# Token products of three tiles with the contraction outside, loads in sixths, low parts on GpSimd, another order of calls

## The chip, the cores and the metric
The kernel runs on one core of a Trainium2 chip, as one launch. The metric is the device time of the launch in microseconds, the median of several runs. The program is one block in which each engine (TensorE, VectorE, ScalarE, GpSimd, SyncE) has its own list of instructions, runs them strictly in order, and waits on semaphores for the others.

## The reference, cut to what matters
A small vision tower: 16 images of 96x96x3, 37 tokens each (36 patches and a class token), 592 rows of 256.

```python
tokens = einsum('bnd,ed->bne', patchify(x, 16), W) + b      # 768 -> 256
h = concatenate([cls, tokens], axis=1) + pos_embedding
n = layernorm(h)
q, k, v = n @ Wq, n @ Wk, n @ Wv            # 8 heads of q, 4 of k and v, 128 wide
q, k = rope(q), rope(k)                     # x * cos + rotate_half(x) * sin
h = h + softmax(causal(q @ k.T * scale)) @ v @ Wo
n = layernorm(h)
probs = softmax(n @ router_w.T); gate = top 4 of 16, the rest 0
h = h + sum over 2 shared experts of gelu(n @ up.T) @ down.T
      + sum over 16 routed experts of gate * (gelu(n @ up.T) @ down.T)
```

## The kernel before
The 592 rows are five tiles of 128 rows (the last has 80). For attention they are six groups of 3, 3, 2 images (111, 111, 74 rows, twice), and for the rope two halves of 296 rows.

**Products with high and low parts.** Apart from the token products, the scores and the products with v, every matmul is made of three: a float32 operand is split into a high part (ScalarE copies it to the float32r type) and a low part (what the rounding left, a subtraction), and `three` adds high x high, high x low, low x high. So each weight and each activation needs a ScalarE copy and a subtraction before TensorE can use it. The subtraction of the attention weights is `qkv_low` on VectorE (L635), four pieces of 128x1024; `qkv_high` on ScalarE (L408) comes first. That of the expert weights is `low_parts` on GpSimd (L372), after `high_parts` on ScalarE (L479).

**Tokens.** `x_sb` holds the patches transposed (six contraction chunks of 128), `wp_sb` the weights (six chunks). `tokens(i)` multiplies tile i over all six chunks, `tokens_added(i)` adds position, bias and class token through a product with `aux_pick` and `aux_parts`, which VectorE prepares in `split_added` (L812 to L817) when `aux_sb` and `auxs_sb` have landed. The loads of tile 0 come in three pieces (chunk 0, chunks 1 and 2, chunks 3 to 5), x on ScalarE's queue and the weights on SyncE's; x of tiles 1, 2 and 3 with 4 come behind on SyncE's queue, then the identity, and then the attention weights in four loads, the second, third and fourth of them behind the mask or the tables of the rope.

**Layernorm.** `norm_stats` (L651 to L655) on VectorE, `inv_std` (L418, L420) on ScalarE, `norm_apply` (L664 to L673) on VectorE. `turn_norm` (L1088) transposes on TensorE, then `turned_high` (L431) on ScalarE and `turned_low` (L681) on VectorE split the result. For the first layernorm (n = 0 to 4) `norm_apply` reads PSUM, for the second (n = 5 to 9) it reads `h` in SBUF.

**Attention.** `project(n)`, n = 0 to 23, makes one head of q or k for one half in one of four banks: six matmuls. ScalarE's `swap(n)` copies its halves crosswise into a ring of three (`swapped`, L450 and L451), GpSimd's `sine(n)` (L356) multiplies that in place, VectorE's `cosine(n)` (L690) writes `qk`, and `rope_add(n)` (L697) adds the two, both in SBUF. `swap(n)` waits for `rope_add(n-3)`, `project(n)` for an earlier `cosine`. `values(g)` and `keep_v(g)` make v. `scores`, `less_max` (VectorE), `exps` (ScalarE), `inv_sum` (VectorE, L725 and L728), `normalise` (GpSimd, L362), `turn_probs`, `keep_pT`, `attend`, `heads_high`, `heads_low`, `project_out`, `add_residual` follow, group by group.

**Experts.** `up(u)`, u = 0 to 35, and `down(e, p)` run on TensorE, with `gelu`, `act_low` and `add_expert` beside them. Split weights stand in a ring of four.

The order of the calls on every engine is written out by hand at the end of each engine's part, and it is this order that the change rewrites. Ahead of the first product `warm_up` runs `WARM_UPS` matmuls on zeros.

## Time and profile before

| | us |
|---|---|
| median of 3 runs | 167.95 |
| lowest and highest | 167.35, 170.6 |
| the profiled execution | 167.21 |
| its span in the profile | 165.0 |
| TensorE busy in it | 152.5 (92%) |
| VectorE busy in it | 133.9 (81%) |

The span is what the profiler shows of that execution, from the first instruction to the last; the time of the execution is 2.2 us longer. The span falls into the loads and token products (to about 21 us), the attention (to about 97 us) and the experts. TensorE's busy time is that of matmuls whose ends are modelled. "Idle before" is the time in which an engine had nothing to do ahead of an instruction, with what ended it.

### The profile page before, as it was taken

To read this page: it belongs to the slowest core of one execution; us is meant where nothing else is said; L and a number is where in the kernel's file an instruction comes from. 1 tells how busy PE (TensorE), PEld (TensorE's weight loads), DVE (VectorE), ACT (ScalarE), POOL (GpSimd) and SP (SyncE) were. 2 spreads that over 40 slices of the span, in tenths; PEclk is the share of its full clock that TensorE was granted. 3 is DMA by queue.
4 is the path that set the end of the run, shared out by engine and by line. 5 is a ranking of instruction groups with operands and counts; after the bars stand their busy time and mean duration, and the time that the engine had idled before them with its cause. 6 is when DMAs were issued, how large, how long until landed. Compare 5 with 4: busy or idle time off the path is not lost.

```text
span 165.0 us, 3245 instructions
## 1 busy us (share of the span) xinstructions
PE 152.5 (92%) x1102; PEld 141.9 (86%) x1102; DVE 133.9 (81%) x340; ACT 95.1 (58%) x230; POOL 55.4 (34%) x58
## 2 busy tenths in 40 slices
PE   7799798999999699999985999999999999999990
PEld 2578587997988598999984999999999999999990
DVE  0266999899889999999997375689699969968893
ACT  3006687997667678559563039867556358365500
POOL 0000025735559364262094000043704633415100
PEclk9999999999999999999998699999999999999999
DMA  5999800000000008990000000000000000000004
GB/s 151 332 353 357 343 1 4 2 2 0 4 0 0 0 0 292 420 422 21 0 0 0 4 0 2 0 6 0 0 0 6 0 0 0 4 0 0 4 0 147
DMA packets 7329, 11.86 MB, mean 72 GB/s; under 512 B 834, under 2 KB 5138, under 8 KB 7186
## 3 DMA queue, kind: packets, MB, share of 16 engines
q1 hardware_dynamic: 6354, 11.14, 18.9%
q10 hardware_dynamic: 960, 0.52, 1.1%
q8 instruction: 9, 0.15, 0.4%
q14 instruction: 6, 0.05, 0.1%
HBM read 11.05 MB, written 0.61 MB: 71 GB/s over the span
## 4 chain that ended last, share of the span: by engine, by line
PE 57%; DVE 20%; ACT 8%; issue 5%; SPq 4%; DMA 4%; DVEq 0%; ACTq 0%
PE bank L1047 46%; DVE qk L697 5%; DMA mask_f<-mask_in 4%; ACT swapped L451 3%; ACT swapped L450 3%; PE bank L1163 3%; DVE h L802 3%; DVE qk L690 2%; DVE hn L673 2%; PE bank L1136 2%; DVE smax L714 2%; SPq L323 2%; PE bank L1069 2%; DVE wo_lo L830 1%; SPq L322 1%
## 5 line engine op out<-in xcount | busy, mean ns | idle before, releaser
L372 POOL TENSOR_TENSOR exp_lo<-ffn_sb,exp_hi 128x512 fp32r<-128x512 f32 x18 | 24.3, 1360 | 45.2 <-ACT exp_hi L479 45.2
L802 DVE SCALAR_TENSOR_TENSOR h<-bank,gate,h 128x256 f32<-128x256 f32 (+1 forms) x80 | 32.6, 472 | 3.0 <-PE bank L1047 2.7
L356 POOL TENSOR_TENSOR swapped<-swapped,sin_sb 128x296 f32<-128x296 f32 x24 | 21.0, 886 | 37.9 <-ACT swapped L451 37.6
L1047 PE MATMUL bank<-exp_hi,act_hi 128*128 128x256 f32 (+1 forms) x90 | 25.4, 282 | 0.0
L1047 PE MATMUL bank<-exp_lo,act_hi 128*128 128x256 f32 (+1 forms) x90 | 25.3, 281 | 0.0
L1047 PE MATMUL bank<-exp_hi,act_lo 128*128 128x256 f32 (+1 forms) x90 | 25.3, 281 | 0.0
L1047 PE MATMUL bank<-hnT_hi,exp_hi 128*128 128x256 f32 (+1 forms) x72 | 22.1, 306 | 0.0
L1047 PE MATMUL bank<-hnT_hi,exp_lo 128*128 128x256 f32 (+1 forms) x72 | 21.5, 298 | 0.0
L1047 PE MATMUL bank<-hnT_lo,exp_hi 128*128 128x256 f32 (+1 forms) x72 | 21.5, 298 | 0.0
L782 DVE TENSOR_TENSOR act_lo<-act,act_hi 128x256 fp32r<-128x256 f32 (+1 forms) x36 | 16.5, 486 | 4.8 <-ACT act_hi L491 4.3
L488 ACT ACTIVATE act<-bank 128x256 f32<-128x256 f32 (+1 forms) x36 | 15.2, 422 | 8.5 <-PE bank L1047 8.0
L479 ACT ACTIVATE exp_hi<-ffn_sb 128x512 fp32r<-128x512 f32 x18 | 11.0, 628 | 11.8 <-PE bank L1047 11.8
L1047 PE MATMUL bank<-hnT_hi,wqkv_hi 128*128 128x296 f32 x48 | 15.3, 319 | 2.4 <-DVE qk L690 1.6
L1047 PEld LDWEIGHTS bank<-exp_hi,act_hi 128*128 128x128 f32 (+1 forms) x90 | 16.3, 181 | 0.1
L1047 PEld LDWEIGHTS bank<-exp_lo,act_hi 128*128 128x128 f32 (+1 forms) x90 | 16.2, 180 | 0.0
L1047 PEld LDWEIGHTS bank<-exp_hi,act_lo 128*128 128x128 f32 (+1 forms) x90 | 16.2, 180 | 0.0
L1069 PE MATMUL bank<-wp_sb,x_sb 128*128 128x256 f32 (+1 forms) x60 | 14.4, 385 | 1.0 <-DMA x_sb<-xT 1.0
L491 ACT ACTIVATE act_hi<-bank 128x256 fp32r<-128x256 f32 (+1 forms) x36 | 15.3, 424 | 0.0
L362 POOL TENSOR_TENSOR probs<-probs,sinv 111x444 f32<-111x444 f32 (+1 forms) x12 | 10.0, 850 | 14.4 <-DVE sinv L728 14.3
L1047 PE MATMUL bank<-hnT_hi,wqkv_lo 128*128 128x296 f32 x48 | 14.4, 299 | 0.0
L1047 PE MATMUL bank<-hnT_lo,wqkv_hi 128*128 128x296 f32 x48 | 14.4, 299 | 0.0
L450 ACT ACTIVATE swapped<-bank 64x296 f32<-64x296 f32 x24 | 10.0, 415 | 7.5 <-PE bank L1047 7.1
(94 smaller groups left out, 377.6 us busy)
## 6 DMA issues: line engine op xcount, KB each, us to landing
ffn_sb<-w_ffn SPq DMA_DIRECT2D x6, 768.0 KB, 9.1
wqkv_sb<-w_qkv SPq DMA_DIRECT2D x4, 512.0 KB, 7.1
wo_sb<-w_o SPq DMA_DIRECT2D x1, 1024.0 KB, 10.1
x_sb<-xT SPq DMA_DIRECT2D x2, 384.0 KB, 6.3
x_sb<-xT SPq DMA_DIRECT2D x1, 624.0 KB, 7.7
out<-h SPq DMA_DIRECT2D x2, 256.0 KB, 2.2
wp_sb<-wpT SPq DMA_DIRECT2D x1, 384.0 KB, 4.6
wp_sb<-wpT SPq DMA_DIRECT2D x1, 256.0 KB, 3.1
```

Source lines behind the costliest of these rows:

```text
L356: nc.gpsimd.tensor_tensor(swapped[:, n % 3, :], swapped[:, n % 3, :], sin_sb[:], ALU.mult).then_inc(qk_sin, 1)
L362: nc.gpsimd.tensor_tensor(quad(probs, g, c), quad(probs, g, c), per_head(sinv, g, c), ALU.mult).then_inc(sc_norm, 1)
L372: nc.gpsimd.tensor_tensor(exp_lo[:, e % SPLIT_RING, :], ffn_sb[:, e, :], exp_hi[:, e % SPLIT_RING, :].bitcast(F32), ALU.subtract).then_inc ...
L450: nc.scalar.activation(swapped[0:64, n % 3, :], ps[64:128, 0:HT], ACT.Copy)
L479: nc.scalar.activation(exp_hi[:, e % SPLIT_RING, :], ffn_sb[:, e, :], ACT.Copy).then_inc(exp_hi_made, 1)
L488: nc.scalar.activation(act[:, r, 0:n], bank[up_bank(u)][:, 0:n], ACT.Gelu).then_inc(act_made, 1)
L491: nc.scalar.activation(act_hi[:, r, 0:n], bank[up_bank(u)][:, 0:n], ACT.Gelu).then_inc(act_hi_made, 1)
L697: nc.vector.tensor_tensor(qk[:, head, half(b)], qk[:, head, half(b)], swapped[:, n % 3, :], ALU.add).then_inc(qk_roped, 1)
L782: nc.vector.tensor_tensor(act_lo[:, r, 0:n], act[:, r, 0:n], act_hi[:, r, 0:n].bitcast(F32), ALU.subtract).then_inc(act_lo_made, 1)
L802: last = nc.vector.scalar_tensor_tensor(h[r, i, :], y, gate[r, i, one], h[r, i, :], ALU.mult, ALU.add)
L1047: last = nc.tensor.matmul(ps, a, b, start=(n == 0 and m == 0), stop=(n == len(pairs) - 1 and m == 2 and not more))
L1069: nc.tensor.matmul(ps, x_sb[:, k, tile(i)], wp_sb[:, k, :], start=(k == 0), stop=False)
```

## The change
1. **Tokens.** Tiles 0, 1 and 2 (`EARLY = 3`) are multiplied together: `tokens_early(k)` does chunk k for the three of them, in three banks, and needs only chunk k of x and of the weights. Tiles 3 and 4 stay as they were.
2. **Loads.** x and weights of the early tiles come in sixths, one chunk each, alternating between SyncE's and ScalarE's queue. `aux_sb` stands behind them on ScalarE's queue, and x of tiles 3 and 4 behind that. `xT` is laid out on the host so that each load has one contiguous run in each partition.
3. **Low parts.** `qkv_low` moves from VectorE to GpSimd, ahead of all `sine` calls.
4. **Warm-up.** Six matmuls for seven.
5. **Order of calls.** It is rewritten on all four engines.

```diff
-WARM_UPS = 7
+WARM_UPS = 6
+EARLY = 3
...
+        def load_chunk(queue, what, k):
+
+            if what == "wp":
+                queue.dma_start(wp_sb[:, k, :], wpT[:, k, :]).then_inc(l_wp[k], 16)
+            else:
+                early = slice(k * EARLY * P, (k + 1) * EARLY * P)
+                queue.dma_start(x_sb[:, early], xT[:, early]).then_inc(l_x[k], 16)
...
-            for k, (c, d) in enumerate(CHUNK_LOADS):
-                sp.dma_start(wp_sb[:, c:d, :], wpT[:, c:d, :]).then_inc(l_wp[k], 16)
+            for k in range(KP):
+                load_chunk(sp, ("wp", "x")[k % 2], k)
             sp.dma_start(auxs_sb[:], aux_sel).then_inc(l_aux, 16)
-            for n, (a, z) in enumerate(((P, 2 * P), (2 * P, 3 * P), (3 * P, T))):
-                sp.dma_start(x_sb[:, :, a:z], xT[:, :, a:z]).then_inc(l_later_x[n], 16)
...
-            for k, (c, d) in enumerate(CHUNK_LOADS):
-                act_e.dma_start(x_sb[:, c:d, 0:P], xT[:, c:d, 0:P]).then_inc(l_x[k], 16)
+            for k in range(KP):
+                load_chunk(act_e, ("x", "wp")[k % 2], k)
             act_e.dma_start(aux_sb[:], aux_w).then_inc(l_aux, 16)
+            for i in range(EARLY, TILES):
+                late_x = slice(KP * P * i, KP * (P * i + TN[i]))
+                act_e.dma_start(x_sb[:, late_x], xT[:, late_x]).then_inc(l_later_x[i - EARLY], 16)
...
+            def qkv_low(n):
+                c = QKV_ORDER[n]
+                cs = slice(c * CHUNK, (c + 1) * CHUNK)
+                pool.wait_ge(qkv_hi_made, n + 1)
+                nc.gpsimd.tensor_tensor(wqkv_lo[:, :, cs], wqkv_sb[:, :, cs], wqkv_hi[:, :, cs].bitcast(F32),
+                                        ALU.subtract).then_inc(qkv_lo_made, 1)
...
+            def tokens_early(k):
+
+                pe.wait_ge(l_wp[k], 16)
+                pe.wait_ge(l_x[k], 16)
+                for i in range(EARLY):
+                    nc.tensor.matmul(token_bank(i)[:, 0:HID], x_sb[:, patches(i, k)], wp_sb[:, k, :], start=(k == 0),
+                                     stop=False)
```

What that makes of the lists is shown at three places. First the head of TensorE's list, where `bank<-wp_sb,x_sb` are token products, `bank<-aux_parts,aux_pick` is `tokens_added` and `bank<-ident,hn` is `turn_norm`. Before:

```order
L1055 MATMUL bank<-zeros 128x512 x7
L1069 MATMUL bank<-wp_sb,x_sb 128x256 x6
L1076 MATMUL bank<-aux_parts,aux_pick 128x256
...
L1088 MATMUL bank<-ident,hn 128x128 x2
L1069 MATMUL bank<-wp_sb,x_sb 128x256 x6
L1076 MATMUL bank<-aux_parts,aux_pick 128x256
L1088 MATMUL bank<-ident,hn 128x128 x4
L1069 MATMUL bank<-wp_sb,x_sb 80x256 x6
L1047 MATMUL bank<-hnT_hi,wqkv_hi 128x296
```

And of the change:

```order
L1078 MATMUL bank<-zeros 128x512 x6
L1085 MATMUL bank<-wp_sb,x_sb 128x256 x18
L1102 MATMUL bank<-aux_parts,aux_pick 128x256 x3
L1094 MATMUL bank<-wp_sb,x_sb 128x256 x6
L1114 MATMUL bank<-ident,hn 128x128 x2
L1102 MATMUL bank<-aux_parts,aux_pick 128x256
L1094 MATMUL bank<-wp_sb,x_sb 80x256 x6
L1102 MATMUL bank<-aux_parts,aux_pick 80x256
L1114 MATMUL bank<-ident,hn 128x128 x4
L1070 MATMUL bank<-hnT_hi,wqkv_hi 128x296
```

The first `tokens_added` has moved from behind 6 token matmuls to behind all 18 of the early tiles, and the transposes of tiles 1 and 2 stand behind the products of tile 4, directly ahead of the first projection.

Second, ScalarE's first computing instructions (`wqkv_hi<-wqkv_sb` is `qkv_high`, `lnv` and `y` are `inv_std`, `h<-bank` is `keep_tokens`, `hnT_hi` is `turned_high`). Before:

```order
L418 ACTIVATE lnv<-vare 128x1
L420 ACTIVATE y<-lnv 128x1
L418 ACTIVATE lnv<-vare 128x1
L420 ACTIVATE y<-lnv 128x1
L408 ACTIVATE wqkv_hi<-wqkv_sb 128x2x512 x2
L418 ACTIVATE lnv<-vare 128x1
L420 ACTIVATE y<-lnv 128x1
L412 ACTIVATE h<-bank 128x256 x2
L431 ACTIVATE hnT_hi<-bank 128x2x128 x3
```

And of the change:

```order
L439 ACTIVATE wqkv_hi<-wqkv_sb 128x2x512 [waits l_qkv0]
L449 ACTIVATE lnv<-vare 128x1 [waits vare_made]
L451 ACTIVATE y<-lnv 128x1 [waits ln_made]
...
L439 ACTIVATE wqkv_hi<-wqkv_sb 128x2x512 [waits l_qkv2]
L443 ACTIVATE h<-bank 128x256 [waits hn_made]
L462 ACTIVATE hnT_hi<-bank 128x2x128 [waits hnT_turned]
L449 ACTIVATE lnv<-vare 128x1 [waits vare_made]
L451 ACTIVATE y<-lnv 128x1 [waits ln_made]
L439 ACTIVATE wqkv_hi<-wqkv_sb 128x2x512 [waits l_qkv1]
L439 ACTIVATE wqkv_hi<-wqkv_sb 128x2x512 [waits l_qkv3]
L462 ACTIVATE hnT_hi<-bank 128x2x128 [waits hnT_turned] x2
```

The copy of the first attention weights stands ahead of the first `inv_std`, and those of the third and fourth ahead of `turned_high` of tiles 1 and 2, where they stood behind.

Third, GpSimd's whole work. Before (`probs` is `normalise`, `exp_lo` is `low_parts`):

```order
L356 TENSOR_TENSOR swapped<-swapped,sin_sb 128x296 x18
L362 TENSOR_TENSOR probs<-probs,sinv 111x444 x3
L356 TENSOR_TENSOR swapped<-swapped,sin_sb 128x296 x3
L362 TENSOR_TENSOR probs<-probs,sinv 111x444
L356 TENSOR_TENSOR swapped<-swapped,sin_sb 128x296 x3
L362 TENSOR_TENSOR probs<-probs,sinv 74x4x74 x2
L362 TENSOR_TENSOR probs<-probs,sinv 111x444 x4
L362 TENSOR_TENSOR probs<-probs,sinv 74x4x74 x2
L372 TENSOR_TENSOR exp_lo<-ffn_sb,exp_hi 128x512 x18
```

And of the change, with the four pieces of 128x1024 ahead and `low_parts` in the tail:

```order
L370 TENSOR_TENSOR wqkv_lo<-wqkv_sb,wqkv_hi 128x2x512 x4
L377 TENSOR_TENSOR swapped<-swapped,sin_sb 128x296 x15
L383 TENSOR_TENSOR probs<-probs,sinv 111x444
...
L377 TENSOR_TENSOR swapped<-swapped,sin_sb 128x296 x3
L383 TENSOR_TENSOR probs<-probs,sinv 74x4x74
L383 TENSOR_TENSOR probs<-probs,sinv 111x444 x2
L393 TENSOR_TENSOR exp_lo<-ffn_sb,exp_hi 128x512 x3
L383 TENSOR_TENSOR probs<-probs,sinv 111x444 x2
L393 TENSOR_TENSOR exp_lo<-ffn_sb,exp_hi 128x512
L383 TENSOR_TENSOR probs<-probs,sinv 74x4x74 x2
L393 TENSOR_TENSOR exp_lo<-ffn_sb,exp_hi 128x512 x14
```

The four `low_parts` that stood together behind the last `normalise` are now three and one, between the `normalise` calls of groups 3, 4 and 5; the first three `normalise` calls no longer stand together either.

## Rows read from the trace of the kernel before

**Rows 1.** Page, busy time and share of the span, instructions
```profile
PE 152.5 (92%) x1102; PEld 141.9 (86%) x1102; DVE 133.9 (81%) x340; ACT 95.1 (58%) x230; POOL 55.4 (34%) x58
```

**Rows 2.** Windows: stretch, its length, busy us by engine, granted clock, DMA, GB/s
```profile
52.00:56.00 4.00, 3.32 (x34) 3.12 (x34) 3.97 (x6) 3.21 (x8) 2.47 (x3) 1.00 0.00 0
56.00:60.00 4.00, 3.12 (x20) 2.88 (x19) 3.78 (x10) 2.39 (x6) 2.75 (x3) 1.00 0.00 0
84.00:88.00 4.00, 2.45 (x19) 1.91 (x17) 3.72 (x7) 2.84 (x9) 4.00 (x4) 1.00 0.00 0
88.00:92.00 4.00, 3.24 (x20) 3.24 (x21) 1.88 (x4) 0.77 (x2) 0.56 (x1) 0.74 0.02 4
92.00:96.00 4.00, 4.00 (x31) 4.00 (x31) 1.85 (x8) 0.41 (x2) 0.00 (x0) 0.84 0.00 0
```

**Rows 3.** Page, DMA issues: KB each, median us from issue to landing
```profile
x_sb<-xT SPq DMA_DIRECT2D x2, 384.0 KB, 6.3
x_sb<-xT SPq DMA_DIRECT2D x1, 624.0 KB, 7.7
```

**Rows 4.** Timeline, start and duration, first token tile and what it waited for
```profile
2.59 2.25 SPq L322 DMA_DIRECT2D x_sb<-xT  x3
7.33 0.29 DVE L812 CAST aux_high<-aux_sb 64x256 fp32r<-64x256 f32 x1 [6.20 <-DMA aux_sb<-aux_w]
8.34 0.42 DVE L817 TENSOR_TENSOR aux_parts<-aux_sb,aux_high 64x256 fp32r<-64x256 f32 x1
9.10 2.75 PE L1069 MATMUL bank<-wp_sb,x_sb 128*128 128x256 f32 x12
9.30 0.43 DVE L651 BATCH_NORM_STATS2 stats<-bank 128x6 f32<-128x256 f32 x1 [0.54 <-PE bank L1076]
```

**Rows 5.** Timeline, the attention weights' splitting and the first projections
```profile
15.26 1.06 ACT L408 ACTIVATE wqkv_hi<-wqkv_sb 128x1024 fp32r<-128x1024 f32 x1 [0.83 <-DMA wqkv_sb<-w_qkv]
...
20.03 3.48 DVE L635 TENSOR_TENSOR wqkv_lo<-wqkv_sb,wqkv_hi 128x1024 fp32r<-128x1024 f32 x3
...
21.47 0.49 PE L1047 MATMUL bank<-hnT_hi,wqkv_hi 128*128 128x296 f32 x1
...
25.81 0.37 PE L1047 MATMUL bank<-hnT_hi,wqkv_hi 128*128 128x296 f32 x1 [0.80 <-ACT h L412]
```

**Rows 6.** By line, GpSimd and VectorE: count, duration ns min/median/max, first and last start
```profile
L356 POOL TENSOR_TENSOR swapped<-swapped,sin_sb x24: 810/822/1584, 23.7 to 62.4; 128x296 f32<-128x296 f32 x24
L372 POOL TENSOR_TENSOR exp_lo<-ffn_sb,exp_hi x18: 1255/1292/1715, 83.6 to 151.7; 128x512 fp32r<-128x512 f32 x18
L697 DVE TENSOR_TENSOR qk<-qk,swapped x24: 452/458/2747, 25.9 to 64.3; 128x296 f32<-128x296 f32 x24
L673 DVE TENSOR_SCALAR hn<-h,mv,rstd x5: 408/412/2376, 74.9 to 98.7; 128x256 f32<-128x256 f32 x4, 80x256 f32<-80x256 f32 x1
```

**Rows 7.** Timeline, GpSimd and VectorE around 52 us
```profile
51.91 1.01 POOL L362 TENSOR_TENSOR probs<-probs,sinv 111x444 f32<-111x444 f32 x1 [0.16 <-DVE sinv L728]
52.88 1.59 POOL L356 TENSOR_TENSOR swapped<-swapped,sin_sb 128x296 f32<-128x296 f32 x2
...
52.05 2.75 DVE L697 TENSOR_TENSOR qk<-qk,swapped 128x296 f32<-128x296 f32 x1
```

**Rows 8.** Timeline, the last transposes of the attention's end
```profile
83.61 4.94 POOL L372 TENSOR_TENSOR exp_lo<-ffn_sb,exp_hi 128x512 fp32r<-128x512 f32 x4
85.77 0.27 DVE L664 TENSOR_SCALAR vyy<-y,vare 128x1 f32<-128x1 f32 x1
86.33 2.38 DVE L673 TENSOR_SCALAR hn<-h,mv,rstd 128x256 f32<-128x256 f32 x1
88.76 0.44 PE L1088 MATMUL bank<-ident,hn 128*128 128x128 f32 x2 [1.90 <-DVE hn L673]
```

**Rows 9.** Page, ScalarE's crosswise copies: busy, mean ns, idle before
```profile
L450 ACT ACTIVATE swapped<-bank 64x296 f32<-64x296 f32 x24 | 10.0, 415 | 7.5 <-PE bank L1047 7.1
```

**Rows 10.** Chain that ended last, one `project_out`: start, duration
```profile
67.52 2.89 PE bank L1047 x24
```

More of the change, by code:

```diff
@@ L876, in _ @@
             wo_low()
+            cosine(9)
             less_max(0, 0)
-            for n in range(9, 12):
-                cosine(n)
+            cosine(10)
+            cosine(11)
             for n in range(9, 12):
@@ L1064, in tokens @@
                 for k in range(KP):
-                    for n, (first, _) in enumerate(CHUNK_LOADS):
-                        if k == first and i == 0:
-                            pe.wait_ge(l_wp[n], 16)
-                            pe.wait_ge(l_x[n], 16)
-                    nc.tensor.matmul(ps, x_sb[:, k, tile(i)], wp_sb[:, k, :], start=(k == 0), stop=False)
+                    nc.tensor.matmul(token_bank(i)[0:TN[i], 0:HID], x_sb[:, patches(i, k)], wp_sb[:, k, :],
+                                     start=(k == 0), stop=False)
             def tokens_added(i):
@@ L1351, in _ @@
             down(6, 2)
-            up(17)
-            up(18)
+            for n in range(14, 19):
+                up(n)
             down(7, 0)
@@ L1368, in _ @@
             down(10, 0)
-            for n in range(24, 27):
+            down(10, 1)
+            for n in range(23, 27):
                 up(n)
-            down(10, 1)
             down(10, 2)
@@ L1378, in _ @@
             down(12, 2)
-            for n in range(27, 30):
+            for n in range(28, 33):
                 up(n)
```

430 lines of the change are left out of this document (213 added, 217 removed).

## The prediction, made before the changed kernel ran
> **What bounds the kernel.** I read the page's busy times first, then the windows by stage, then the waits and the timeline where TensorE stands still. TensorE is busy 152.5 of 165.0 us [rows 1], so at most about 12 us can go without taking work from it, and the change takes none but one warm-up matmul. The reader should see in the windows where the gaps are: 0.80 us ahead of 25.81 [rows 5], 0.68 and 0.88 us in 52 to 60, 1.55 and 0.76 us in 84 to 92 [rows 2]; behind the last, the granted clock is 0.74 and 0.84 for two windows of 4 us [rows 2]. A clock at half (1.2 GHz for 2.4) for a share s of a window gives a mean of 1 - s/2: s is 0.52 and 0.32, so 3.4 us ran at half the clock, and half of that, 1.7 us, is lost. I found no other gap of that size between the loads (to 21 us) and the last sums. So the question is which of these gaps the new order closes, and what the head costs.
>
> **The two stalls of VectorE.** A `rope_add` takes 458 ns and one took 2747; `norm_apply` of the second norm takes 412 ns and one took 2376 [rows 6]. Both long ones lie under a run of GpSimd instructions without a gap: the `rope_add` of 52.05 ended at 54.80, when GpSimd had gone from 51.91 to 54.47 through one `normalise` and two `sine`; the `hn` of 86.33 ended at 88.71, when four `low_parts` ended at 88.55 [rows 7, 8]. Neither lacked data. The small `vyy` of 85.77 beside the same run took its 0.27 us [rows 8], so it is not every VectorE instruction: those with two SBUF inputs, and wide float32 ones from SBUF to SBUF, wait until GpSimd pauses. The first cost 2.3 us of VectorE's time, the second 1.96 us, on which TensorE's 1.90 us of idleness hangs [rows 8], and behind that the slow clock. The Trainium skill (SBUF — State Buffer, "Who interferes with whom") says that GpSimd and VectorE share a port pair as an exclusive lock, taken by whichever instruction issues first. The trace agrees that it is a lock, and shows more: VectorE's instruction stood through two or three of GpSimd's, not one. By the page's rule alone the `hn` would have waited for one instruction of at most 1.3 us.
>
> **The head: tokens and loads, 0 us.** Bytes ahead of a load decide when it lands. Before, x of tiles 1 and 2 were issued from 2.59 on, 0.65 us apart, and landed 6.3 us later in the median, so around 9.2 with 1874 KB ahead of or in them on average; the 624 KB behind, issued near 3.95, landed near 11.65 [rows 3, 4] at 2690 KB: 0.35 MB/us. With the new order the six pairs of 320 KB end at 1920 KB: 9.3 us. A pair's six matmul records for three tiles take 0.69 us (12 in 2.75, [rows 4]), less than the 0.94 us in which a pair lands, so TensorE follows the loads and is through at 10.0. `aux_sb` now stands behind all of them, at about 10.0 for 7.3; `split_added` needs 1.43 us (7.33 to 8.76, [rows 4]), so tile 0 is complete at 11.7, for 9.3 before: **2.4 us later**, with tiles 1 and 2 right behind. So VectorE's first `norm_stats` is late, and `inv_std(0)` later still, because `qkv_high(0)` stands ahead of it on ScalarE and waits for its load. The second of these loads landed at 15.26 [rows 5] and has the same 3.92 MB ahead of or in it now; the first has 3.18, so 13.1 at 0.35 MB/us. I get `inv_std(0)` at 14.6, `hn` of tiles 0, 1, 2 at 15.7, 17.6, 18.7. Next on ScalarE: the third and fourth loads (4.75 and 5.27 MB, as before) at 17.6 and 19.1; the copies take 1.06 [rows 5] and end at 20.2; only then come `turned_high(1)` and `(2)`, 21.0, and `turned_low(2)` 21.5. TensorE's transposes stand in time (tile 4 done at 19.4). **First projection 21.6, as before (21.47, [rows 5])**: term 0, bounds -1.0 (if the longer runs of the new x layout load faster) and +2.0 (if the clock falls in TensorE's gaps between 4 and 12.4 us, or tile 0 comes later).
>
> **Low parts on GpSimd, -0.9.** VectorE loses 4 instructions, 3.48 us of them at 20.03 to 23.51 [rows 5], on the path. With `inv_std(3)` and `(4)` at 22.0 and 22.4 (behind `turned_high` and two `keep_tokens` on ScalarE), both `norm_apply` are through at 24.2, the fourth and fifth transposes stand together, and `project(3)` starts at 24.9 for 25.81 [rows 5]. On GpSimd, a width of 296 takes 822 ns, 512 takes 1292 [rows 6], so 2.18 ns a column, and 1024 takes 2.4 us: the four end at 16.6, 19.0, 21.4 and 23.8, each a projection or more ahead of its use (`project(6)` needs the third, `values(0)` the fourth, at 28). `sine(0)` can begin at 23.8, for 23.7 [rows 6]. So the move has cover, as long as `sine` follows without a backlog. What it does not give is VectorE's whole 3.5 us: from 25 to 33 us ScalarE's `swap` calls (two copies of 0.415 us, [rows 9], 0.86 with the gap between) set the pace, and `rope_add(1)` now stands behind `cosine(3)` and `turned_low(3)`, so that `swap(4)` comes later by 0.7 us. At `rope_add(11)` I have VectorE 0.5 us behind the old time and TensorE 0.9 ahead.
>
> **The middle, -0.6.** The first three `normalise` no longer make one run, and `rope_add` meets a single GpSimd instruction at a time. Worth up to 1.56 us of TensorE (52 to 60, [rows 2]); since VectorE is 0.5 late there, and bounds are 0 and -1.5, I take -0.6.
>
> **The end of the attention, -1.8 and -1.7.** The four `low_parts` are drawn forward: 0 to 2 ahead of `normalise(4, ...)`, 3 ahead of `normalise(5, ...)`. When `norm_apply(6)` and `(7)` come, behind two residual sums, I have GpSimd just done (4.5 us of it after `inv_sum(4,0)`, by 1.0 for a `normalise` of 444 columns, two thirds for 296, and 1.29 for `low_parts`, against 4.7 us of VectorE). Two `project_out` stand together (2.89 us each, [rows 10]) and cover the chains. Of 2.3 us of gaps I leave 0.5, so -1.8; and a gap that short is not followed by a slow clock in this trace (the 0.88 us before 57 were not, [rows 2]), so -1.7. Bounds: 0 and -4.
>
> **New waits, +0.9.** `low_parts(2)` waits for the last scores and may start just ahead of `norm_apply(5)`: up to one of 1.29 us, taken as 0.5. Among the experts, `up(8)` needs the fifth expert's low part, whose high part waits for `down(1,2)`, and one `down` less stands between: between 0 and one `low_parts` of 1.29, near the lower end, +0.4. The rest of the experts is TensorE's work without gaps, whatever the order: 0. One warm-up less: 0, hidden by the loads.
>
> **Sum.** 0 - 0.9 - 0.6 - 1.8 - 1.7 + 0.9 = -4.1 against the profiled execution's 167.21: 163.1. The median of the runs shown is 0.74 above it and their lowest 0.14, so I add 0.4: **163.5**.
>
> **Rivals.** (a) The head loses what the end gains. For: tile 0 is 2.4 us later, and TensorE stands with short bursts up to 12.4. The clock at half through the products of tiles 3 and 4 (5.5 us of work, twice the 2.75 of [rows 4]) costs up to 2.75 us, of which about 2 arrive: 165.5. Against: ScalarE has its own wait until 19.85. Chance 0.17. (b) The stall at the end only moves: another run of GpSimd meets `norm_apply(6)` or `(7)`; then -3.5 falls away, 167. For: my margin there is 0.2 us. Chance 0.20. (c) Backlog on GpSimd, the other side: if `swap`, `sine` and `rope_add` meet so that every `rope_add` (and `ident_b`, a cast from SBUF) waits for the next `sine` to end, the ring of three goes at 0.82 + 0.46 = 1.28 us a head for ScalarE's 0.86. Twelve heads cost 5 us, all 24 cost 10: 168.6 or 173.6. It decides from about 8 heads on. The rule of the skill on the same page speaks for it, since `rope_add` has two SBUF inputs; by it alone each meeting costs a part of 0.82 us. Against: the row's median is 458 ns with GpSimd busy in most of those stretches, and only one of 24 was long [rows 6]. Chance 0.11. (d) The forecast: 0.52, own range 162 to 165.
>
> **Numbers.** A run of this kernel can tell about 2% (3.4 us) from nothing: the line is at 164.6. Faster: most of (d) and a little of (a), 0.51. Slower (above 171.3): half of (c), 0.05. Range: from 161.5 (the head's -1.0 and the whole middle) to 168.5 (through (b), and the milder (c)).
>
> **What would show it.** Right: the first projection within 0.7 us of 21.5, `project(3)` before 25.2, no `rope_add` and no `hn` above 1.3 us, a granted clock of 1.00 from 84 to 96, and the first `up` about 4 us earlier. Wrong: a granted clock under 1 before 20 us; `inv_std(0)` before 13 (then the head is a gain); a run of GpSimd over `norm_apply(6)` or `(7)`; `rope_add` at 1.2 us many times.

## The result: 159.06 us, and where the 8 us went

The changed kernel takes 159.06 us (four runs, 158.81 to 159.44) against 168.29 us for the kernel before (four runs, 167.35 to 170.6). The ratio is 0.947, with a 95% interval of 0.942 to 0.952. The profiled execution took 159.16 us with a span of 157.2, against 167.21 and 165.0: 8.05 us less. The forecast was 163.1 for the profiled execution and 163.5 for the median, so the direction was right and the gain was about twice as large as worked out.

The medians lie 9.2 us apart, 1.2 more than the profiled executions. TensorE's granted clock (1 is full speed) tells why: the kernel before has spells at half the clock, and not always the same number. It ran 30 more times beside the experiments. The 17 executions with a mean clock of 0.975 to 0.980 took 168.09 to 169.82 us, the 13 with 0.986 or more took 166.11 to 168.95 (medians 169.0 and 167.4). The profiled execution before belongs to the second kind (0.99) and holds one such spell; the trace of `c_loads` below, with a mean of 0.978, holds two. All four runs of the changed kernel have 0.997 or more. So about 1 us of the gain in the medians is one more slow spell that the kernel before has in more than half of its executions. Ratios leave out executions more than 1.5% above the fastest of their kernel, medians only three that took 216, 252 and 837 us.

The page of the changed kernel: busy time, share of the span, and instructions.

```profile
PE 150.4 (96%) x1101; PEld 140.9 (90%) x1101; DVE 125.3 (80%) x336; ACT 95.5 (61%) x230; POOL 63.6 (40%) x62
```

TensorE's instructions are those of before less one warm-up [rows 1]. Its busy time fell by 2.2 us (152.54 to 150.36), which is close to what a stretch at half the clock adds (1.7 us, below); 5.6 us are idleness that is gone, and 0.25 lies outside the span. The waits tell which. First the kernel before: what TensorE waited for, us in total, times, longest.

```profile
PE bank L1088 <- DVE hn L673: 1.9, 1, 1.9
PE bank L1047 <- DVE qk L690: 1.6, 2, 0.9
PE bank L1055 <- DVE zeros L807: 1.2, 1, 1.2
PE bank L1088 <- DVE hnT_lo L681: 1.0, 1, 1.0
PE bank L1069 <- DMA x_sb<-xT: 1.0, 2, 0.8
PE bank L1047 <- ACT h L412: 0.8, 1, 0.8
```

And the changed kernel, the whole list:

```profile
PE bank L1078 <- DVE zeros L835: 1.2, 1, 1.2
PE bank L1070 <- DVE hnT_lo L709: 1.1, 1, 1.1
PE bank L1189 <- ACT probsT L497: 0.2, 1, 0.2
```

All that is left between the first warm-up and the last product is one wait of 1.1 us ahead of the first projection and one of 0.2 behind a softmax. The windows show the same (stretch, its length, busy us by engine, granted clock, DMA share, GB/s; to be laid beside [rows 2]):

```profile
52.00:56.00 4.00, 4.00 (x36) 3.98 (x34) 3.83 (x12) 3.72 (x9) 2.96 (x4) 1.00 0.02 4
56.00:60.00 4.00, 3.93 (x31) 3.78 (x31) 3.96 (x10) 3.77 (x10) 3.05 (x5) 1.00 0.12 12
84.00:88.00 4.00, 4.00 (x36) 4.00 (x35) 2.15 (x7) 0.51 (x3) 0.00 (x0) 1.00 0.02 4
88.00:92.00 4.00, 4.00 (x37) 4.00 (x36) 2.95 (x11) 1.96 (x5) 0.00 (x0) 1.00 0.00 0
```

Where in the program the time was won can be read from the start of the same call of TensorE in the two traces (us from the start of the span):

| TensorE starts | before | changed | difference | won since the line above |
|---|---|---|---|---|
| `tokens_added(0)` | 8.91 | 12.70 | +3.79 | |
| `project(0)` | 21.47 | 21.11 | -0.36 | 0.36 (head) |
| `project(3)` | 25.81 | 23.99 | -1.82 | 1.46 (fourth tile) |
| `scores(3,1)` | 64.86 | 61.41 | -3.45 | 1.63 (middle) |
| `project_out(3)` | 88.95 | 83.34 | -5.61 | 2.16 |
| `up(0)` | 97.19 | 89.61 | -7.58 | 1.97 (with the line above: end of attention) |
| last `down` | 160.39 | 152.74 | -7.65 | 0.07 (experts) |

Behind the last `down` another 0.15 us is won within the span, and 0.25 us outside it: 8.05 in all. Ahead of `project_out(3)` and of the last `down` stands the same work in both, but for the warm-up. Ahead of `scores(3,1)` the new order has four records more and ahead of `up(0)` four fewer, so those two lines are good to about 0.5 us: at equal work `up(0)` is some 7.1 us ahead, and about 0.5 of the 7.65 comes among the experts. TensorE's idle time in the same stretches fell from 3.50 to 2.48 us in the head, from 0.92 to 0 by the fourth tile, from 1.64 to 0.16 in the middle, and from 2.31 to 0.27 between `scores(3,1)` and `project_out(3)`; behind that it is 0 in both up to the last `down`.

The difference of 0.36 us in the head isn't to be read. Two kernels below have the head of the kernel before unchanged, and their first projection starts at 21.92 and 21.93 us for 21.47; one has that of the changed kernel, and starts it at 21.55 for 21.11. So where the program starts its first projection is known to about 0.5 us from one trace, and a difference at a later call holds that scatter too, unless it is counted from the first projection on.

**The head.** Timeline of the changed kernel: start, duration, engine, line and operation, in brackets the idle time before it.

```profile
3.91 9.14 PE L1085 MATMUL bank<-wp_sb,x_sb 128*128 128x256 f32 x36
...
9.41 0.29 DVE L840 CAST aux_high<-aux_sb 64x256 fp32r<-64x256 f32 x1 [8.28 <-DMA aux_sb<-aux_w]
...
12.60 1.06 ACT L439 ACTIVATE wqkv_hi<-wqkv_sb 128x1024 fp32r<-128x1024 f32 x1 [5.70 <-DMA wqkv_sb<-w_qkv]
...
12.70 0.70 PE L1102 MATMUL bank<-aux_parts,aux_pick 128*128 128x256 f32 x3
...
13.21 0.43 DVE L679 BATCH_NORM_STATS2 stats<-bank 128x6 f32<-128x256 f32 x1 [2.36 <-PE bank L1102]
...
18.50 1.06 ACT L439 ACTIVATE wqkv_hi<-wqkv_sb 128x1024 fp32r<-128x1024 f32 x1 [0.27 <-DMA wqkv_sb<-w_qkv]
...
20.31 0.74 DVE L709 TENSOR_TENSOR hnT_lo<-bank,hnT_hi 128x256 fp32r<-128x256 f32 x2
...
21.11 0.40 PE L1070 MATMUL bank<-hnT_hi,wqkv_hi 128*128 128x296 f32 x1 [1.14 <-DVE hnT_lo L709]
```

The 18 token products of the early tiles are 36 records and took 9.14 us, without a pause, because TensorE and not the loads set their pace: 36 of 0.229 us are 8.2, and the clock was at half until 6.20. The statistics of tile 0 start at 13.21 for 9.30 before [rows 4], and the first projection still starts no later (21.11 for 21.47), since it waits for the low parts of tiles 1 and 2, not for tile 0.

**VectorE's stalls.** By line in the changed kernel: `rope_add`, then `norm_apply` of the second norm (duration ns least/median/most, first and last start).

```profile
L725 DVE TENSOR_TENSOR qk<-qk,swapped x24: 450/458/819, 24.2 to 60.9; 128x296 f32<-128x296 f32 x24
```

```profile
L701 DVE TENSOR_SCALAR hn<-h,mv,rstd x5: 408/411/415, 71.5 to 91.6; 128x256 f32<-128x256 f32 x4, 80x256 f32<-80x256 f32 x1
```

The instructions of 2747 and 2376 ns [rows 6] have no counterpart. How near GpSimd came to `norm_apply(5)` the timeline shows:

```profile
68.28 2.50 POOL L393 TENSOR_TENSOR exp_lo<-ffn_sb,exp_hi 128x512 fp32r<-128x512 f32 x2
...
71.51 0.41 DVE L701 TENSOR_SCALAR hn<-h,mv,rstd 128x256 f32<-128x256 f32 x1
...
71.79 1.28 POOL L393 TENSOR_TENSOR exp_lo<-ffn_sb,exp_hi 128x512 fp32r<-128x512 f32 x1 [1.02 <-PE bank L1162]
```

It starts 0.7 us behind the end of one pair of `low_parts` and 0.28 us ahead of the next, which begins while it still runs, and it takes its usual 0.41. The longest meeting that is left is among the experts, where an `act_lo` (0.50 us in the median) takes 1.45 under one `low_parts`; TensorE waits for none of it.

### The profile page after: what moved, and what is told of

The parts are those of the page before. It is cut to its first block, busy times and chain, and to the rows that moved or that the text cites. A ratio compares the mean times of both kernels' runs of the same rounds, so it can differ in the third digit from the quotient of the medians.

```text
span 157.2 us, 3252 instructions
## 1 busy us (share of the span) xinstructions
PE 150.4 (96%) x1101; PEld 140.9 (90%) x1101; DVE 125.3 (80%) x336; ACT 95.5 (61%) x230; POOL 63.6 (40%) x62
## 4 chain that ended last, share of the span: by engine, by line
PE 83%; DVE 12%; issue 2%; ACT 1%; DVEq 0%
PE bank L1070 62%; PE bank L1085 6%; PE bank L1162 4%; PE bank L1189 4%; DVE h L830 2%; PE bank L1078 2%; PE bank L1174 2%; DVE qk L718 1%; PE bank L1158 1%; PE bank L1213 1%; DVE stats L679 1%; DVE hn L701 1%; DVE qk L725 1%; DVE ssum L753 1%; PE bank L1114 1%
## 5 line engine op out<-in xcount | busy, mean ns | idle before, releaser
L377 POOL TENSOR_TENSOR swapped<-swapped,sin_sb 128x296 f32<-128x296 f32 x24 | 20.0, 837 | 12.5 <-ACT swapped L482 12.2
L810 DVE TENSOR_TENSOR act_lo<-act,act_hi 128x256 fp32r<-128x256 f32 (+1 forms) x36 | 18.4, 527 | 5.6 <-ACT act_hi L522 4.9
L1070 PE MATMUL bank<-hnT_hi,exp_lo 128*128 128x256 f32 (+1 forms) x72 | 21.5, 299 | 0.0
L1070 PE MATMUL bank<-hnT_lo,exp_hi 128*128 128x256 f32 (+1 forms) x72 | 21.5, 298 | 0.0
L370 POOL TENSOR_TENSOR wqkv_lo<-wqkv_sb,wqkv_hi 128x1024 fp32r<-128x1024 f32 x4 | 9.4, 2368 | 13.5 <-ACT wqkv_hi L439 13.5
L1070 PEld LDWEIGHTS bank<-hnT_hi,exp_hi 128*128 128x128 f32 x72 | 13.5, 188 | 0.1
L1070 PEld LDWEIGHTS bank<-hnT_lo,exp_hi 128*128 128x128 f32 x72 | 13.6, 188 | 0.0
```

The source lines that it names most:

```text
L370: nc.gpsimd.tensor_tensor(wqkv_lo[:, :, cs], wqkv_sb[:, :, cs], wqkv_hi[:, :, cs].bitcast(F32), ALU.subtract).then_inc(qkv_lo_made, 1)
L377: nc.gpsimd.tensor_tensor(swapped[:, n % 3, :], swapped[:, n % 3, :], sin_sb[:], ALU.mult).then_inc(qk_sin, 1)
L810: nc.vector.tensor_tensor(act_lo[:, r, 0:n], act[:, r, 0:n], act_hi[:, r, 0:n].bitcast(F32), ALU.subtract).then_inc(act_lo_made, 1)
L1070: last = nc.tensor.matmul(ps, a, b, start=(n == 0 and m == 0), stop=(n == len(pairs) - 1 and m == 2 and not more))
```

## The experiments

Three theories were to be told apart. The first is the prediction's: VectorE stands through runs of GpSimd instructions, and the new order breaks those runs. The second is that moving `qkv_low` off VectorE is what pays, and the third that the loads and token products pay. Eleven kernels were run in twelve runs. Times are medians; each ratio is against runs of the kernel before on the same chip (its medians there were 168.31 to 168.66). Milestones, as "the last `down` starts", are from one profiled execution of each.

### The end of the attention: is it the unbroken run of GpSimd?

The changed kernel with all its `low_parts` behind the last `normalise`, where they stood before:

```diff
-            for n in range(0, 3):
-                low_parts(n)
             normalise(4, 0)
             normalise(4, 1)
-            low_parts(3)
             normalise(5, 0)
             normalise(5, 1)
-            for n in range(4, 18):
+            for n in range(0, 18):
                 low_parts(n)
```

> The changed kernel with GpSimd's low_parts(0) to (3) all behind the last normalise, as before the change. Theory 1 (the placing of low_parts removed the stall): the four run over norm_apply(6) or (7), an hn of 1.5 us or more comes back, TensorE waits 1 to 2 us and the clock may fall: 160.5 to 162.5 us. Rival (VectorE's and TensorE's new order at the end did it): within 0.5 us of 159.1.

163.67 us (163.11 to 164.59), ratio 0.978 [0.964, 0.992], slower than the 160.5 to 162.5 expected; in its trace the last `down` starts 4.4 us later than in the changed kernel, 0.4 of it already at the first projection, which the edit doesn't touch. Its timeline:

```profile
75.51 3.10 POOL L383 TENSOR_TENSOR probs<-probs,sinv 111x444 f32<-111x444 f32 x4 [6.74 <-DVE sinv L753]
78.57 4.94 POOL L393 TENSOR_TENSOR exp_lo<-ffn_sb,exp_hi 128x512 fp32r<-128x512 f32 x4
...
80.56 3.10 DVE L698 TENSOR_SCALAR hn<-h,mv,rstd 128x256 f32<-128x256 f32 x1
...
83.72 0.44 PE L1111 MATMUL bank<-ident,hn 128*128 128x128 f32 x2 [1.65 <-DVE hn L698]
...
84.13 0.41 DVE L698 TENSOR_SCALAR hn<-h,mv,rstd 128x256 f32<-128x256 f32 x1
```

The stall is back, and longer than before: an `hn` of 0.41 us takes 3.10 and ends at 83.66, when the run of GpSimd has ended at 83.51. The next `hn`, with GpSimd idle, takes 0.41 again. TensorE idles 1.65 and 0.45 us for it, and its clock falls behind that (a spell at half from 85.48 to 88.89). The two waits and the spell (1.7 us) make 3.8 of the 4.0 us that are left. So the placing of the four `low_parts` is worth about 4 us in this kernel, half of the 8.

The other way round, the kernel before with its second `low_parts` held back until `norm_apply(7)`, the one that was stalled there, is through:

```diff
                 pool.wait_ge(exp_hi_made, e + 1)
+                if e == 1:
+                    pool.wait_ge(hn_made, TILES + 3)
```

> The kernel before with one wait more: GpSimd's low_parts(1) waits until norm_apply(7) is done, so that no run of four low_parts lies over it. Theory 1 (the hn of 2.38 us was held by GpSimd's run, and TensorE's idle 1.9 us and the 3.4 us at half the clock followed from it): that hn takes about 0.4 us, or 1.3 at most, the granted clock stays 1.00 from 84 to 96, and the time falls by 3 to 3.6 us, to 164 to 165. Rival (the clock falls anyway, by the shorter gaps before): down by 1.5 to 2, to 166. Rival (hn was late for another cause): no change.

165.12 us (164.45 to 166.04), ratio 0.983 [0.974, 0.992]. Its profiled execution is the one of 216 us, and its trace can't be read against the others, so the same kernel ran once more:

> The kernel of d_break_run again, for its profile. Theory 1 (GpSimd's run held the hn, and the idle time and the half clock hang on it): the hn of tile 2 takes 0.4 us, TensorE's gap ahead of its transpose is under 0.6 us for 1.90, the granted clock is 1.00 from 84 to 96, and the last matmul is 3 to 3.6 us earlier than in the kernel before. Rival (another cause of the late hn): the row of 2.38 us stays.

165.88 and 164.12 us, ratio 0.985 [0.963, 1.007]. Its timeline:

```profile
85.66 1.27 POOL L374 TENSOR_TENSOR exp_lo<-ffn_sb,exp_hi 128x512 fp32r<-128x512 f32 x1
...
88.38 0.41 DVE L675 TENSOR_SCALAR hn<-h,mv,rstd 128x256 f32<-128x256 f32 x1
...
88.96 1.29 POOL L374 TENSOR_TENSOR exp_lo<-ffn_sb,exp_hi 128x512 fp32r<-128x512 f32 x1 [2.03 <-DVE hn L675]
```

With the run cut, `hn` takes 0.41 us. From the first `project_out` (2.04 us later than in the kernel before) to `up(0)` (1.42 earlier) 3.4 us are won. Those 2 us of delay come from elsewhere: 0.45 us from the head, 1.6 from the middle. After the two gaps there, which are still in this kernel, the clock fell. Windows of the same trace, columns as above:

```profile
54.00:58.00 4.00, 2.47 (x20) 2.05 (x19) 3.93 (x9) 2.53 (x6) 1.22 (x3) 1.00 0.00 0
58.00:62.00 4.00, 4.00 (x16) 3.77 (x16) 2.58 (x6) 1.52 (x4) 2.65 (x3) 0.57 0.02 4
```

The mean of 0.57 is a clock at half (1.2 GHz) from 58.03 to 61.45. In the trace of before the same two gaps were followed by full speed [rows 2]. So by the trace the repair is worth 3.4 us, the stall and the slow clock behind it, while the ratio of 0.983 makes 2.9 us of the 168.3; a slow spell that turns up elsewhere, as in this trace, can take such a part of it.

### The middle: the `rope_add` of 2.75 us

The kernel before with two `rope_add` ahead of the `inv_sum` that sets GpSimd's run free:

```diff
             cosine(17)
-            inv_sum(1, 0)
             rope_add(16)
             rope_add(17)
+            inv_sum(1, 0)
```

> The kernel before with two VectorE calls exchanged: rope_add(16) and (17) ahead of inv_sum(1,0), so that they come before GpSimd's run of normalise and sine. Theory 1 (that run blocked rope_add(17) for 2.3 us and TensorE's two gaps of 0.68 and 0.88 us followed): no rope_add above 1.3 us, the gaps go, and 1 to 1.5 us are gained: 166.5 to 167 us against 168 of the kernel before. Rival (TensorE is late there because of VectorE's load as a whole): under 0.4 us.

165.72 us (165.70 to 169.11), ratio 0.989 [0.977, 1.001]: from the median alone it isn't settled. The trace settles it. The longest `rope_add` is 1126 ns for 2747, and these are its windows:

```profile
52.00:56.00 4.00, 3.83 (x40) 3.57 (x38) 3.90 (x11) 3.74 (x9) 2.42 (x4) 1.00 0.00 0
56.00:60.00 4.00, 4.00 (x26) 3.98 (x27) 3.94 (x9) 3.14 (x8) 2.75 (x4) 1.00 0.00 0
```

TensorE's idle time in the 8 us is 0.17 us, for 1.56 [rows 2]. In this trace the first projections were 0.45 us later than before, `scores(3,1)` 1.20 earlier: 1.65 us are won in the middle, the whole gap of 1.56. At the end of this trace the 1.9 us wait for `hn` and the slow clock (87.03 to 90.45) stand as before.

### The low parts of the attention weights, alone and in the new order

The kernel before with nothing changed but the engine of `qkv_low`:

```diff
-                dve.wait_ge(qkv_hi_made, n + 1)
-                nc.vector.tensor_tensor(wqkv_lo[:, :, cs], ...
+                pool.wait_ge(qkv_hi_made, n + 1)
+                nc.gpsimd.tensor_tensor(wqkv_lo[:, :, cs], ...
...
+            for n in range(0, 4):
+                qkv_low(n)
             for n in range(0, 18):
                 sine(n)
```

> The kernel before with one part of the change: qkv_low on GpSimd ahead of all sine calls, every other call where it was. Theory 1: project(3) starts 1 us earlier or more, and the gaps of 52 to 60 us and at 88 stay, since GpSimd's two runs stay: 166 to 167 us. Rival (VectorE's 4.7 us go through to the end): 163.5. Rival (GpSimd's backlog blocks rope_add): 168 to 170, with rope_add rows of 1.2 us.

168.62 us over ten runs (166.3 to 171.03), ratio 0.996 [0.991, 1.002]: nothing, where 166 to 167 was expected. Its timeline:

```profile
20.50 0.54 DVE L675 TENSOR_SCALAR hn<-bank,mv,rstd 128x256 f32<-128x256 f32 x1
...
25.18 0.39 ACT L421 ACTIVATE h<-bank 128x256 f32<-128x256 f32 x1
25.60 1.59 POOL L363 TENSOR_TENSOR swapped<-swapped,sin_sb 128x296 f32<-128x296 f32 x2
...
25.71 0.37 PE L1046 MATMUL bank<-hnT_hi,wqkv_hi 128*128 128x296 f32 x1 [1.15 <-POOL wqkv_lo L356]
```

The `hn` of the fourth tile is there at 21.04, yet `project(3)` starts at 25.71, as in the kernel before (25.81, [rows 5]). It waits for a bank, which `keep_tokens(3)` on ScalarE (the `h` of 25.18) empties, behind three `swap`. The row names GpSimd, whose fourth low part ended at nearly the same time, but the kernel `l_four` below starts `project(3)` at 24.56 while that subtraction is still running, so it was ScalarE. The third and fourth `qkv_low` end at 25.63, so the first `sine` starts at 25.60 for 23.7 [rows 6], and `project(7)` is 1.1 us later than before. That 1.1 us is still there at `project_out(3)`. It is regained behind it, because this trace has the gap of the end and no slow clock:

```profile
88.00:92.00 4.00, 2.11 (x18) 2.11 (x19) 3.00 (x4) 1.19 (x3) 1.69 (x2) 1.00 0.00 0
92.00:96.00 4.00, 4.00 (x37) 4.00 (x36) 2.21 (x8) 0.41 (x2) 0.00 (x0) 1.00 0.01 4
```

The changed kernel with only `qkv_low` taken back to VectorE:

```diff
             norm_apply(1)
+            qkv_low(0)
             norm_apply(2)
...
             turned_low(2)
+            for n in range(1, 4):
+                qkv_low(n)
             norm_apply(3)
```

> The changed kernel with qkv_low back on VectorE: piece 0 between norm_apply(1) and norm_apply(2), pieces 1 to 3 behind turned_low(2), as before the change. Theory 1 (the move is worth what it frees ahead of project(3)): 1.2 us of VectorE ahead of the first projection and 3.5 ahead of norm_apply(3) come back, of which TensorE sees 0.5 and then 1.5 to 3: 161 to 162.5 us. Rival (VectorE is the bound of the whole attention, so all 4.7 us come back): 163.5 to 164. Rival (VectorE has slack, the order did it): within 1 us of 159.1.

163.43 us (162.77 to 164.94), ratio 0.976 [0.966, 0.985]. That is more than the 161 to 162.5 expected, and nearly the figure of the rival by which all of VectorE's 4.7 us come back. Its timeline:

```profile
21.34 3.48 DVE L661 TENSOR_TENSOR wqkv_lo<-wqkv_sb,wqkv_hi 128x1024 fp32r<-128x1024 f32 x3
...
25.29 0.55 DVE L699 TENSOR_SCALAR hn<-bank,mv,rstd 128x256 f32<-128x256 f32 x1
```

```profile
25.89 0.44 PE L1115 MATMUL bank<-ident,hn 128*128 128x128 f32 x2 [1.39 <-DVE hn L699]
```

Here the 3.48 us lie wholly on the path: the new order has `norm_apply(3)` and `(4)` behind them and ahead of `project(3)`, which comes at 27.04 for 23.99, 3.05 us later. And the loss stays. It is 3.1 us at `scores(3,1)` and 3.4 at the last `down`, since nowhere behind does TensorE wait for anything that could take it up. So what the trace shows is a delay of 3.1 us by the fourth tile, and not VectorE as the bound of the whole attention.

### The loads and token products, alone and in the new order

The kernel before with the new loads, layout, `tokens_early` and six warm-ups, and its own order of calls otherwise:

```diff
-            tokens(0)
-            tokens_added(0)
-            tokens(1)
-            tokens_added(1)
-            tokens(2)
-            tokens_added(2)
+            for n in range(0, 6):
+                tokens_early(n)
+            for n in range(0, 3):
+                tokens_added(n)
             turn_norm(0)
             tokens(3)
```

> The kernel before with the loads, the token products and the six warm-ups of the change, every other call where it was. Theory 1 (the new loads and the contraction outside are no gain by themselves; tile 0 is complete at 13 us for 9, so the first projection is later by about 1 us): 168.5 to 169.5 us. Rival (faster loads carry through): 167 or less.

170.08 us (169.54 to 170.67), ratio 1.012 [1.005, 1.019]: alone, this part loses, and more than expected. Windows of its head:

```profile
14.00:16.00 2.00, 0.00 (x0) 0.00 (x0) 1.39 (x6) 0.41 (x2) 0.00 (x0) 1.00 1.06 386
16.00:18.00 2.00, 1.93 (x8) 1.69 (x9) 1.79 (x8) 1.27 (x4) 0.00 (x0) 0.74 1.09 423
18.00:20.00 2.00, 2.00 (x7) 1.53 (x6) 1.93 (x5) 1.95 (x7) 0.00 (x0) 0.50 0.72 286
```

and its timeline:

```profile
16.07 0.41 PE L1108 MATMUL bank<-ident,hn 128*128 128x128 f32 x2 [2.40 <-DVE hn L690]
16.32 4.44 PE L1088 MATMUL bank<-wp_sb,x_sb 128*128 128x256 f32 x12
```

The three tiles end together, and the next call of TensorE is the transpose of tile 0, whose norm has only begun. TensorE stands 2.40 us, the clock falls to half (16.95 to 20.36), and the next twelve records take 4.44 us for 2.75 [rows 4]. `project(0)` comes 2.8 us late and the last `down` 2.8 us late. The new order puts the products of tile 3 into that hole.

The changed kernel with the old loads, tokens tile by tile and seven warm-ups:

```diff
-            for n in range(0, 6):
-                tokens_early(n)
-            for n in range(0, 3):
-                tokens_added(n)
+            tokens(0)
+            tokens_added(0)
+            tokens(1)
+            tokens_added(1)
+            tokens(2)
+            tokens_added(2)
```

> The changed kernel with the loads, token products by tile and seven warm-ups of the kernel before. Theory 1 (the load part gives nothing by itself; the first projection hangs on TensorE's token work and the norms, 21 us either way): 159 to 160 us. Rival (the sixths and the contraction outside are what fills TensorE's load gaps of 1.8 us, and all of it goes through to the end): 161 or more.

160.28 us (159.91, 160.28, 160.6), ratio 0.956 [0.944, 0.969]. `project(0)` starts 0.96 us later than in the changed kernel and the last `down` 0.92. So in the new order the same part gains about 1 us (1.2 by the medians); the first projection alone shifts by up to 0.5 us from trace to trace, as said above.

### The order of calls alone

Both parts undone in the changed kernel (`qkv_low` on VectorE, old loads), which leaves the new order:

> The changed kernel with its new order alone: loads and token products by tile as before, and qkv_low on VectorE. Theory 1 (the parts add up in this order: 3.4 us for the low parts by a_low_dve, 0.9 for the loads by j_old_loads): the last matmul at 157.1 us, 163.8 to 165 us in all, so the order by itself gives 3 to 4 us. Rival (the parts need each other, so each undone part costs more alone than together): 162 to 163.5. Rival (they hide each other's loss): above 165.5.

164.70 us (163.94 to 165.82), ratio 0.979 [0.972, 0.985]. `project(3)` starts at 28.66 and `project(7)` at 34.92, since VectorE's subtractions stand ahead of the fourth tile, and the gaps there are followed by a slow clock (half from 29.57 to 32.98). Windows:

```profile
24.00:28.00 4.00, 2.54 (x16) 1.86 (x14) 3.85 (x9) 1.21 (x3) 1.89 (x1) 1.00 0.00 0
28.00:32.00 4.00, 3.50 (x19) 3.50 (x20) 2.79 (x8) 3.39 (x9) 2.13 (x3) 0.70 0.02 4
```

Four kernels with the new order now make a square (medians, us):

| new order | `qkv_low` on VectorE | on GpSimd | difference |
|---|---|---|---|
| old loads | 164.70 | 160.28 | -4.42 |
| new loads | 163.43 | 159.06 | -4.37 |
| difference | -1.27 | -1.22 | |

The intervals of these medians are 1 to 3 us wide, so the differences are good to about 1 us; the traces give 3.4 and 0.9 for the two steps to the changed kernel. In this order the two parts add up: 3.6 us for the order (168.29 to 164.70), 4.4 for GpSimd, 1.2 for the loads. The 3.6 is the least certain of them: the profiled executions of the two kernels, each with one slow spell, are only 1.4 us apart. In the old order the same parts gave 0 and lost 1.8. They are worth something because the order puts them on the path and then takes them off it: `norm_apply(3)` and `(4)` ahead of `project(3)`, `keep_tokens(3)` ahead of the `swap` calls.

### Can the old order be mended with single edits?

The kernel before with `qkv_low` on GpSimd, `keep_tokens(3)` directly behind `swap(0)`, the two `rope_add` moved and the run of GpSimd cut:

```diff
             swap(0)
-            swap(1)
-            swap(2)
             keep_tokens(3)
+            swap(1)
+            swap(2)
```

> The kernel before with four small edits and no other reordering: qkv_low on GpSimd (b_low_pool), ScalarE's keep_tokens(3) ahead of swap(1) and swap(2), rope_add(16) and (17) ahead of inv_sum(1,0) (e_ropes), and the wait in low_parts(1) (d_break_run). Theory 1 (TensorE's gaps add up one by one: about 1 for project(3), 1.6 in the middle, 3.4 at the end): 161.5 to 163.5 us. Rival (with GpSimd's backlog at the head the first is lost and others grow): 164 to 166.

164.25 us (163.6 to 165.56), ratio 0.979 [0.972, 0.985]. `project(3)` starts at 24.56, 1.25 us earlier than before; but `project(7)` at 30.87, 1.56 later. TensorE's row ahead of that:

```profile
28.50 0.38 PE L1049 MATMUL bank<-hnT_hi,wqkv_hi 128*128 128x296 f32 x1 [1.19 <-DVE qk L695]
```

and what stands on GpSimd and VectorE before it:

```profile
26.06 2.59 POOL L363 TENSOR_TENSOR swapped<-swapped,sin_sb 128x296 f32<-128x296 f32 x3
...
26.99 0.99 DVE L702 TENSOR_TENSOR qk<-qk,swapped 128x296 f32<-128x296 f32 x1 [0.79 <-POOL swapped L363]
```

GpSimd's fourth subtraction ends at 26.1, the three `sine` behind it are a run from 26.06 to 28.65, `rope_add(0)` takes 0.99 us under it, and `cosine(2)`, which stands behind it on VectorE, frees the bank of `project(6)` late; another 0.8 us go ahead of `turn_norm(4)`. The clock falls for the same 3.4 us (31.32 to 34.73). This is the backlog on GpSimd, the prediction's rival (c), in an order in which ScalarE's last `qkv_high` ends at 22.5, for 19.6 in the changed kernel. There `qkv_high(2)` and `(3)` are drawn ahead on ScalarE, and the four subtractions end at 23.3.

### Two tries to beat the changed kernel

One wait is left, 1.1 us for `hnT_lo` ahead of the first projection. In one try ScalarE's copies of tiles 1 and 2 went ahead of the last `qkv_high`, and VectorE's `norm_stats(4)` behind their low parts:

```diff
             qkv_high(2)
-            qkv_high(3)
             turned_high(1)
             turned_high(2)
+            qkv_high(3)
```

> The changed kernel with ScalarE's qkv_high(3) behind turned_high(1) and (2), and VectorE's norm_stats(4) behind turned_low(1) and (2). Theory 1 (TensorE stands 1.4 us ahead of the first projection for turned_low(2), and VectorE's 0.8 us of norm_stats(4) are in that path): first projection 0.4 us earlier, and TensorE's work carries it to the end: 158.5 to 158.8 us. Rival (the fourth low part, and with it sine(0), comes later and gives it back): 159.1 or above.

159.90 us over six runs (159.45 to 160.09), ratio 0.952 [0.947, 0.956]: not better than 0.947. In the other only the seventh warm-up is back (`WARM_UPS = 7`):

> The changed kernel with seven warm-up matmuls for six. Theory 1 (in the changed kernel the granted clock rose at 6.2 us, in the kernel before at 4.6; a seventh closes TensorE's gap ahead of the first token product, and the first six of those run at full clock): the clock rises by 5 us and the time falls by 0.2 to 0.6. Rival (when the clock rises varies from run to run, 4.4 in a_low_dve with six and 6.2 in b_low_pool with seven): no change, within 0.2.

159.36 us over six runs (159.15 to 160.14), ratio 0.949 [0.945, 0.954]: the same as the changed kernel. The warm-up taken away was worth nothing that the runs can tell. No kernel of the study beats the changed one; with TensorE busy for 150.4 of 157.2 us there is little left to win by order.

## Why the prediction was right in direction and short by half in size

**Head, forecast 0, measured -0.36,** which one trace can't tell from 0. Within its bounds, but by luck: two errors cancel. The step "a pair's six matmul records for three tiles take 0.69 us (12 in 2.75)" is a slip of arithmetic: six of twelve in 2.75 are 1.37 us, more than the 0.94 in which a pair lands. So TensorE and not the loads limits the early tiles; they are through at 13.0 instead of 10.0 (the clock at half until 6.20, about 1.1 us, was left out too), and tile 0 is complete at 13.2, not at 11.7. Against that `aux_sb` and the attention weights came earlier than worked out (12.60 for 13.1, the fourth load 18.50 for 19.1). What mattered was that the path to the first projection goes over the transposes and low parts of tiles 1 and 2, and that step held: it forecast `turned_low(2)` done at 21.5, it was 21.05.

**Fourth tile, forecast -0.9, measured -1.82 with the head's -0.36.** The mechanism held (both `norm_apply` free of VectorE's 3.48 us); `inv_std(3)` ended at 21.3 instead of 22.0, on the earlier loads. The trace of `b_low_pool` adds what the prediction didn't say: the subtraction alone would have bought nothing, because `keep_tokens(3)` came as late. And the term's label misleads. "Low parts on GpSimd, -0.9" is what this part and the order bring together by `project(3)`; the part itself is worth 4.4 us by the medians in the new order (3.4 in the trace), which without it would be 2.85 us later at `project(3)` than the kernel before.

**Middle, forecast -0.6, measured -1.63.** This is the first step that failed in size. The prediction had the bound, 1.56 us of idle TensorE [rows 2], and the right cause, and took 0.6 of it since "VectorE is 0.5 late there". `e_ropes` shows that breaking the meeting gives the whole gap, 1.65 us. And VectorE wasn't late in the changed kernel. The prediction had it 0.5 us behind the old time at `rope_add(11)`; that instruction started at 39.93 us for 40.42 before, 0.5 ahead, and `rope_add(17)` at 51.57 for 52.05. So the term took off 1 us for a delay that did not exist.

**End of the attention, forecast -1.8 and -1.7 with 0.5 back for `norm_apply(5)`, measured -4.1** (from `scores(3,1)` to `up(0)`). At equal work it is about 3.6. Both mechanisms were right. `f_one_run` puts the same cause back and loses 4.0 behind the head: TensorE's waits of 1.65 and 0.45 us on the stalled `hn`, and the slow clock. The 0.5 us of gaps kept back are not in the trace.

**New waits, forecast +0.9, measured none.** This is the second step that failed. `low_parts(2)` could have met `norm_apply(5)` and missed it by 0.28 us; among the experts, the time from `up(0)` to the last `down` is 63.2 us before and 63.1 after, and at equal work the section is 0.5 us shorter. Where those 0.5 us come from is open. Both waits were priced at a third or more of their worst case though no row showed them; that TensorE has no idle time at all from `up(0)` to the last `down` shows that neither came.

**Offset, forecast +0.4, measured -0.1.** The four runs of the changed kernel have their median 0.10 us below the profiled one; the runs spread over 0.6 us, for 3.3 us of the kernel before. The 0.4 came from the spread of the kernel before, much of which is slow spells (above) that the changed kernel doesn't have.

Term by term, the changed kernel beat the forecast by 0.4 us in the head, 0.6 by the fourth tile, 1.0 in the middle, 0.6 at the end of the attention, 1.0 by the new waits that didn't come, and 0.4 behind the last `down`, where nothing was forecast: together the distance of 159.16 to 163.1. The middle and the new waits make half of it.

**The range was wrong at its low end**, 161.5. It took the head's 1.0 us and the whole middle, and left the +0.9 of new waits and the 0.5 of kept gaps in place, as if they were certain. The prediction had itself counted every gap: 0.80, 0.68 and 0.88, 1.55 and 0.76, and 1.7 of slow clock, 6.4 us together. All of them closed gives 160.8, and with the head's bound 159.8. That should have been the low end of the profiled execution, since each edit aimed at one of these gaps. It came out 0.7 us below even that: 0.4 us were won behind the last `down`, and 1.46 by the fourth tile, where the counted gap was 0.80; the head gave 0.6 less than its bound.

**The rivals.** (a), the head loses by the slow clock, did not come about here, but `c_loads` is this rival: 2.40 us of gap and a clock at half through tile 3. In the new order the products of tile 3 stand where that gap was. (b), the stall only moves, is what `f_one_run` puts back, at 163.7 where the prediction had 167. (c), the backlog on GpSimd, is seen in part in `b_low_pool` and `l_four`, at `rope_add(0)` of 1.0 us; in the changed kernel no `rope_add` exceeds 0.82 us.

## What to carry to other kernels

Where one engine is busy for over 90% of the span, list its gaps and what follows each (here a slow clock): the list is both the estimate and the far end of the range, and here each gap that an edit closed came through in full (1.6 us in the middle for 1.56, 4.1 at the end of the attention for 2.3 and 1.7). The worth of an edit is that in its order of calls: moving work off an engine gave nothing in the old order and about 4 us in the new one, a load scheme lost 1.8 and then gained about 1, so estimate the order first and the parts in it. And where a VectorE instruction from SBUF to SBUF is on the path, let no run of GpSimd instructions lie over it: keep them single, with a pause behind each. In this kernel that removed both long stalls.
